# Order of products in a split-precision MLP on one core: a hoisted down product, halved waits, a carried block and a reordered tail

## The reference

```
attn      = softmax((x @ Wq) @ (x @ Wk).T / 16)
attn_out  = (attn @ (x @ Wv)) @ Wp + bp
cms_out   = gelu(attn_out @ cW1 + cb1) @ cW2 + cb2 + one_hot(code)   # 256 -> 1024 -> 256
modifier  = gelu([attn_out, cms_out] @ mW1 + mb1) @ mW2 + mb2        # 512 -> 1024 -> 256
x         = clip(x + cms_out + modifier, 0, 1)
for 3 adapter layers, weights chosen by the batch's role (3 roles):
    y = x + gelu(x @ W_down + b_down) @ W_up + b_up                  # 256 -> 128 -> 256
    x = layernorm(y) * gamma + beta
```

## Time and profile before

| | us |
|---|---|
| median of 3 runs (369.72 to 371.65) | 370.35 |
| the profiled execution, its own time | 371.1 |
| its span, first to last instruction | 369.3 |
| PE busy | 351.5 (95% of the span) |
| DVE busy | 197.3 (53%) |
| ACT busy | 166.0 (45%) |
| POOL busy | 61.4 (17%) |

### The profile page before, as it was taken

How to read it: one execution, slowest core, us unless ns; L and a number is a source line. 1 busy time by engine, 2 the same in 40 slices (tenths; PEclk the granted TensorE clock), 3 DMA queues, 4 the chain that set the end, 5 groups by cost and what they waited for, 6 DMA issues and landing times.

```text
span 369.3 us, 6638 instructions
## 1 busy us (share of the span) xinstructions
PE 351.5 (95%) x2248; PEld 284.1 (77%) x2248; DVE 197.3 (53%) x477; ACT 166.0 (45%) x333; POOL 61.4 (17%) x94
## 2 busy tenths in 40 slices
PE   6889999999999999999999999999999999999984
PEld 5776688686786877788776767877889898989852
DVE  5165365322243746744536665554578777454574
ACT  2554685333533536433325453443355554533421
POOL 2710400000040101001321110103322125100121
PEclk9999999999999999999999999999999999999998
DMA  6459993383010124120057796602847442297001
GB/s 231 149 217 297 127 113 73 81 174 89 2 43 14 34 85 111 58 88 0 28 173 214 197 261 227 189 30 76 223 129 189 156 115 87 70 284 303 16 2 44
DMA packets 30646, 46.14 MB, mean 125 GB/s; under 512 B 4779, under 2 KB 15348, under 8 KB 30612
## 3 DMA queue, kind: packets, MB, share of 16 engines
q1 hardware_dynamic: 28852, 41.72, 42.4%
q0 software_dynamic: 1392, 3.80, 3.4%
q10 hardware_dynamic: 368, 0.20, 0.2%
HBM read 43.60 MB, written 4.48 MB: 130 GB/s over the span
## 4 chain that ended last, share of the span: by engine, by line
PE 71%; DVE 6%; SPq 5%; issue 5%; ACT 4%; DMA 4%; POOL 3%; DVEq 0%; POOLq 0%
PE bank L312 9%; PE bank L314 9%; PE bank L313 9%; PE bank L1336 7%; PE bank L1341 6%; PE bank L1337 6%; PE bank L1261 4%; PE bank L1380 3%; DMA mixed_w<-packed_w 3%; PE bank L1359 3%; SPq L528 2%; PE bank L1254 2%; PE bank L1235 2%; POOL xr L641 2%; ACT h_full L747 1%
## 5 line engine op out<-in xcount | busy, mean ns | idle before, releaser
L747 ACT ACTIVATE h_full<-bank,bias 128x512 f32<-128x512 f32 (+1 forms) x80 | 48.2, 602 | 117.5 <-PE bank L314 107.2
L974 DVE TENSOR_TENSOR h_lo<-h_full,h_hi 128x512 fp32r<-128x512 f32 (+1 forms) x80 | 47.3, 591 | 68.1 <-ACT h_hi L751 65.6
L669 POOL TENSOR_TENSOR rstd<-moments,minus_half 128x1 f32<-128x1 f32 x39 | 24.3, 623 | 176.4 <-DVE moments L1028 176.4
L751 ACT ACTIVATE h_hi<-h_full 128x512 fp32r<-128x512 f32 (+1 forms) x80 | 43.7, 546 | 2.5
L1020 DVE TENSOR_TENSOR window_y<-bank,window_x 128x256 f32<-128x256 f32 x39 | 16.5, 423 | 42.0 <-PE bank L1359 35.0
L1336 PE MATMUL bank<-h_hi,c_hi 128*128 128x512 f32 (+1 forms) x80 | 31.3, 400 | 0.7 <-ACT h_hi L751 0.6
L1336 PE MATMUL bank<-h_hi,m_hi 128*128 128x512 f32 (+1 forms) x80 | 31.1, 398 | 0.4 <-ACT h_hi L751 0.3
L312 PE MATMUL bank<-at_hi,m_hi 128*128 128x512 f32 (+1 forms) x80 | 30.0, 375 | 0.0
L312 PE MATMUL bank<-at_hi,c_hi 128*128 128x512 f32 (+1 forms) x80 | 29.4, 368 | 0.0
L314 PE MATMUL bank<-at_lo,m_hi 128*128 128x512 f32 (+1 forms) x80 | 28.3, 353 | 0.0
L313 PE MATMUL bank<-at_hi,m_lo 128*128 128x512 f32 (+1 forms) x80 | 28.2, 352 | 0.0
(11 more groups left out here) (216 smaller groups left out, 718.2 us busy)
## 6 DMA issues: line engine op xcount, KB each, us to landing
adapter_w<-packed_w SPq DMA_DIRECT2D x48, 256.5 KB, 3.6
adapter_rows<-packed_rows SPq DMA_DIRECT2D x36, 256.0 KB, 4.1
mixed_w<-packed_w SPq DMA_DIRECT2D x12, 256.5 KB, 4.9
stage<-in_L_cond_mW SPq DMA_DIRECT2D x6, 512.0 KB, 5.1
stage<-in_L_cond_cW SPq DMA_DIRECT2D x4, 512.0 KB, 4.2
last_w<-packed_w SPq DMA_DIRECT2D x2, 769.5 KB, 6.1
up_bias<-in_L_cond_b_up SPq DMA_DIRECT2D x12, 128.0 KB, 5.4
adapter_rows<-packed_rows SPq DMA_DIRECT2D x24, 64.0 KB
```

The lines of the kernel that those rows point to most:

```text
L669: pool.tensor_tensor(slot.rstd[:, :], slot.moments[:, 1:2], minus_half[:, :], ALU.pow)\
L747: act.activation(h_full[:, n % 2, rows], bank[n % 2][:, rows], ACT.Gelu, bias=bias[:, b:b + 1])\
L751: act.activation(h_hi[:, n % 2, rows], h_full[:, n % 2, rows], ACT.Copy).then_inc(h_hi_ready, 1)
L974: dve.tensor_tensor(h_lo[:, n % 2, rows], h_full[:, n % 2, rows], h_hi[:, n % 2, rows].bitcast(F32), ALU.subtract).then_inc(h_lo_ready, 1)
```

## The change

Five edits:

1. In `core`, `D 7` moves ahead of `Ha 8`, so that it stands directly behind `D 6`, and `C` with it; `Ha 8` and `Ha 9` now both lie behind `C`.
2. DVE starts each `cms_lo` half when its own `cms_hi` half is there, and PE waits for each half before the matmul that reads it.
3. For a short group (g = 3, 4: `CARRIED`) step `H 0` is taken out of its own group and put between `D 14` and `D 15` of the group before. `E` of that earlier group then stands directly behind its `F`.
4. The number that hidden products, gelus and high parts wait for becomes `all_but_last(g, n)`: for n = 0 it leaves out the last block of the group before. For n > 0 it is what it was.
5. In the tail `last_up(one, 2)` moves from behind `last_down(one, 2)` to behind `last_turn(two_, 1)` and `last_residual(two_, 1)`.

Otherwise the loops are only rewritten to walk one list `steps` of (group, step).

```
+        def all_but_last(g, n):
+            return max(PRIMED + 2 * HB * g + n - 1, PRIMED)
...
-        core += [("D", HB - 2), ("Ha", HB), ("D", HB - 1), ("C", 0), ("Ha", HB + 1), ("Hb", HB), ("Hb", HB + 1)]
+        core += [("D", HB - 2), ("D", HB - 1), ("C", 0), ("Ha", HB), ("Ha", HB + 1), ("Hb", HB), ("Hb", HB + 1)]
...
+        CARRIED = [g for g in range(1, NM) if GROUPS[g][1] < GR]
+        steps = []
+        for g in range(NM):
+            for step in core:
+                if step == ("H", 0) and g in CARRIED:
+                    continue
+                if step == ("D", 2 * HB - 1) and g + 1 in CARRIED:
+                    steps.append((g + 1, ("H", 0)))
+                steps.append((g, step))
...
@@ scalar: part H @@
-                    act.wait_ge(h_lo_ready, PRIMED + 2 * HB * g + max(n - 1, 0))
+                    act.wait_ge(h_lo_ready, all_but_last(g, n))
...
-                    act.wait_ge(h_used, PRIMED + 2 * HB * g + max(n - 1, 0))
+                    act.wait_ge(h_used, all_but_last(g, n))
...
@@ vector: part C @@
-                        dve.wait_ge(cms_hi_ready, VB * (g + 1))
+                        dve.wait_ge(cms_hi_ready, VB * g + vb + 1)
...
@@ vector: loop over steps @@
-                    if g > 0 and step == ("H", 0):
-                        part("E", 0, g - 1)
+                if g > 0 and g not in CARRIED and step == ("H", 0):
+                    part("E", 0, g - 1)
+                if g + 1 in CARRIED and step == ("F", 0):
+                    part("E", 0, g)
...
@@ tensor: part H @@
-                        pe.wait_ge(gelu_done, PRIMED + 2 * HB * g + max(n - 1, 0))
+                        pe.wait_ge(gelu_done, all_but_last(g, n))
...
-                        pe.wait_ge(cms_lo_ready, VB * (g + 1))
                         for k in ks:
+                            pe.wait_ge(cms_lo_ready, VB * g + k - VB + 1)
                             ins = pe.matmul(o, high(slice(w + k * H, w + k * H + P)), cms_lo[:, k - VB, rows],
                                             start=False, stop=(k == k_all - 1))
...
@@ tensor: tail @@
             last_down(one, 2)
-            last_up(one, 2)
             for layer in range(1, LAYERS):
                 last_turn(two_, layer)
                 last_residual(two_, layer)
+                if layer == 1:
+                    last_up(one, 2)
                 last_down(two_, layer)
```

More of the change, by code:

```diff
@@ L670, in after @@
                         .then_inc(slot.rstd_ready, 1)
[L672 to L679, removed]
+            for wave, step in steps:
+                if step in SPOT:
+                    before(wave, SPOT[step])
+                    after(wave, SPOT[step])
+                if wave == 0 and step == ("F", 0):
+                    pool.wait_ge(z_done, 3)
+                    gather(3)
             for tail, layer in LAST_NORMS:
@@ L824, in _ @@
             stores = []
[L825 to L845, removed]
+            for g, step in steps:
+                part(*step, g)
+                if g == 0 and step == ("H", 1):
+                    attention_part("B", 1)
+                if step in SPOT:
+                    after(g, SPOT[step])
+                if step in HALF:
+                    half(g, HALF[step])
+                if g == NM - 1 and step == ("H", HB + 2):
+                    last_part("down", last[0], 0)
+                if g == NM - 1 and step in (("D", 1), ("D", 3), ("D", 5)):
+                    act.wait_ge(roles_known, 1)
+                    stores.append(store_batches(act, len(stores), range(WIN // 2, WIN)))
+                if g == 0 and step in CHUNK_AT:
+                    chunks(CHUNK_AT[step], CHUNK_AT[step] + 1)
+                if g == 0 and step == ("H", 6):
+                    act.wait_ge(acol_turned, 1)
+                    act.activation(acol[:, :], bank[6][:, 0:21], ACT.Copy).then_inc(acol_ready, 1)
+                if step in ATTENTION.get(g, {}):
+                    attention_part(*ATTENTION[g][step])
             one, two_, three = last
@@ new lines, in _ @@
+            for g, step in steps:
+                part(*step, g)
+                if g == 0 and step == ("H", 1):
+                    attention_part("A", 1)
+                if step in SPOT:
+                    after(g, SPOT[step])
+                if step in HALF:
+                    half(g, HALF[step])
+                if g == NM - 1 and step == ("D", HB):
+                    pe.wait_ge(cms_copied, VB * NM)
+                    pe.wait_ge(last[0].loaded, 16 * last[0].loads)
+                    pe.wait_ge(x1_ready, x1_needed(LAST[0]))
+                    last_down(0, 0)
+                    last_first_sum(0)
+                if g == NM - 1 and step == ("D", HB + 2):
+                    last_residual(0, 0)
+                    last_up(0, 0)
+                if g == NM - 1 and step == ("D", 2 * HB - 2):
+                    last_turn(0, 1)
+                    last_residual(0, 1)
+                if g == 0 and step == ("H", 6):
+                    pe.wait_ge(at_hi_ready, VB * AHEAD)
+                    pe.wait_ge(at_lo_ready, VB * AHEAD)
+                    pe.wait_ge(adapter_in, 16 * ADAPTER_DMAS)
+                    pe.transpose(bank[6][:, 0:21], acol_rows[:, :], ident[0:21, 0:21]).then_inc(acol_turned, 1)
+                if g == 0 and step == ("H", 7):
+                    down_biases()
+                if step in ATTENTION.get(g, {}):
+                    attention_part(*ATTENTION[g][step])
```

61 lines of the change are left out of this document (31 added, 30 removed).

## The result

The changed kernel takes **366.75 us** (median of 4 runs, 365.68 to 367.36), the kernel before in the same session 370.72 (369.72 to 371.65): ratio 0.9873, 95% interval 0.9838 to 0.9908. So it is faster, by 4.0 us (1.1%) by the medians and by 1.3% by this ratio; the two estimates differ by about 0.2%, within the interval. The forecast was 365.5 in a range of 364.0 to 367.4. The profiled execution is the run of 367.36, with a span of 365.6.

What follows compares the result with a forecast made beforehand. TensorE, busy 95% of the span, was taken as the bound, so only its waits could be won. Terms of 1.4, 0.7, 0.1, 0.6, 0.4, 0.3, 0.55 and 0.8 summed to 4.85 us: 365.5 us, range 364.0 to 367.4.

Steps and rivals of the forecast that it cites:

- The sum: All gains from group 0 to the tail added: 4.85 us, giving 365.5 us.
- Groups 0, 1 and 2: Around Hb 8, the earlier D 7 and C and the halved waits save 1.4, 0.7 and 0.1 us.
- Group 3 and the transitions: Waits in Hb 8, D 8 go: 0.6; D 0 of groups 3, 4 stops waiting: 0.3 and 0.55 us.
- Group 4: Up to last_down(0, 0) TensorE gains 0.4 us; the rest becomes a wait for the first tail window's loads.
- The tail: With last_up(one, 2) moved, TensorE no longer waits there for a gelu: 0.8 us.
- The halves in group 4: Halved waits for cms_lo could be met anyway once D 7 is hoisted; no separate gain counted.
- Rival 1: D 7 waits and the carried H 0 gains nothing: 2.6 us less gain, 367.8 us; chance 0.12 in part or whole.
- Rival 2: In the transitions the norm waits less on POOL, and loads land early: 364.2 us; chance 0.06.
- Rival 3: Group 4's hoisted D 7 releases loads that delay those for last_down(0, 0): 3 us lost, 368.6 us; chance 0.06.
- Rival 4: New half-clock stretches of TensorE in short groups and tail, 1.7 us each; four give 372.3 us; chance 0.02.

Runs made afterwards that it cites:

- hoist alone: The kernel before with only D 7 and C moved ahead of Ha 8: 367.77 us against 370.28, ratio 0.9954.
- carried alone: The kernel before with only H 0 of groups 3 and 4 moved ahead of D 15: 370.21 us, ratio 0.9985.

## Why the prediction was right, and where it was not

- **The sum.** Without the start and the fetch, where no edit lies, the profile of the whole change gains 4.76; the forecast had 4.85. That it comes so close is in part luck: 0.13 and 0.15 too much in the first transition and in group 4 are nearly made good by 0.15 too little in the tail and 0.06 in groups 0 to 2, and the profile of the repeat has 4.10. The 4.0 of the medians lies lower: the two profiles lost 0.40 and 1.38 in the start, and one 0.61 at the fetch, which the forecast took as constant. The repeat in another session, 367.88, lies above the range, so that the first four runs fell inside is in part luck too; over all 15 runs the median is 367.04.
- **Groups 0, 1 and 2**: 1.4, 0.7 and 0.1 summed, 1.41, 0.72 and 0.13 measured, and by the parts that were named: hoist for 0, halves for 1. No wait of D 7 for `h_hi` appeared, so the window work and the bias products cover it.
- **Group 3 and the transitions**: 0.3 + 1.15 summed, 0.17 + 1.13 measured. The mechanism is the one forecast: D 0's wait became a wait for E. The 0.3 of the first was counted to the product. That starts 270.45 - 268.96 = 1.49 earlier than before, D 8 of group 2 1.24 earlier, so 0.25 were gained up to there. It forgot that the matmuls behind a new wait start late as well; 0.08 went so. From group 3 to 4 the product came 314.34 - 313.65 = 0.69 behind E's end and comes 0.10 behind it now; less the same 0.08 that is 0.51, where 0.55 was taken.
- **Group 4: the term that was mis-sized.** The step read: "TensorE gains 330.84 - 330.4 = -0.4". It took the landing as fixed at 5.3 after the issue. Behind the same issue the runs landed at 5.3 to 6.2. In the five profiles that have hoist, halves and window 13's loads as in the change, the term measured 0.25, 0.14, -0.35, -0.56 and -0.63. The slack of 0.4 of the kernel before covers a part of that scatter only: with its order here, the two profiles with landings of 5.8 and 6.0 lost 0.25 and 0.40. Hoist and halves used up the slack. That TensorE would meet a wait for DMA was right.
- **The tail**: 0.8 summed, 0.95 measured. The new order gave 0.85 to the product of `two_`, and the step overlooked that this product no longer follows a late start, which takes 0.11 more off it.
- **The halves in group 4.** The text took the halved waits as met anyway in groups 0, 3 and 4 once D 7 is hoisted, as no window work lay in group 4. The norm of window 12 lies there on DVE. The hoist alone brought D 8 forward by 0.17 with a wait of 0.29 for `cms_lo` left, both by 0.64. The sum didn't suffer, as the term ended at the landing.
- **Rival 1** (D 7 waits, E takes all) is out: no wait of D 7, and the transitions gained. **Rival 2** (more than the sum) came by itself in three other kernels: 0.3 in a transition where POOL was quick, which the change has no part in. **Rival 3**, loads in each other's way: the landing did slip, over the 5.5 us named as its sign in one profile of the whole change (6.2), but it slips without the earlier release too (5.8 and 6.0); its price of 3 us is excluded (its time, 370.35 - 1.85, is 368.5 and not 368.6), 0.2 isn't. The Trainium skill (DMA: Bandwidth & Descriptors, Queues, rings and completion order) gives ring order within a queue; that the landings with and without the earlier release overlap agrees with it, and doesn't prove it.
- **Rival 4**, the clock: no stretch of low clock came between group 0 and TensorE's last product in any of the 14 profiles. The known one was there in 11 of 14 profiles of all kernels, absent in three, double in one. It was there with the change and without it, and one such stretch cost 1.56, where 1.7 was forecast.

**To carry on.** Where an edit lets the bound engine come earlier, list what it meets next and how much that scatters: a gain that ends at a transfer's landing is worth only what a late landing leaves of it. Splitting the semaphore so that the first user waits only for what it reads brought back 0.53 to 0.66 in three profiles (the POOL luck taken off). Measure parts by stretches between fixed instructions: repeats there were within 0.1 us where neither a landing nor POOL had a part, while whole times of one kernel scatter by 2 to 6 us. Two parts that shorten the same wait don't add up, as hoist and halves in group 0; before two parts are said not to add up, look whether one of them had luck, as carried alone.

## What the runs showed of the hardware beside that

- TensorE's granted clock fell to 0.50, its 1.2 GHz level, in group 0 behind the tiny bias products while the engine was busy all the time before and in it (row below), in 11 of 14 profiles; the same instructions ran at full clock, 2.4 GHz, in three. The stretch of 3.4 us cost 1.56. The Trainium skill (TensorE: Matmul & The Clock Gate, HAM oscillation) ties the low clock to gaps between matmuls; the busy rows, 3.70 us in 3.70 before the fall and 3.40 in 3.40 in the stretch, show none, so the rows don't bear that out here. The windows view of before, columns as in the earlier trace rows:

```profile
59.20:62.90 3.70, 3.70 (x29) 3.48 (x30) 2.51 (x5) 2.26 (x3) 0.00 (x0) 1.00 0.07 18
```

- The reciprocal root on POOL, 128x1 elements, takes either 0.55 to 0.60 or 0.85 to 0.87 us in the norms ahead of the tail, in the same place of the same kernel; 5 to 10 of its 39 calls there were long in each profile. Where a chain to TensorE goes through it, that is 0.3 us. What makes a call long stays open.
- The work ahead of group 0, the gathers of `x` among it, put its D 0 anywhere from 41.6 to 43.6 us, about as much as the largest part of this change was worth.
